# Three single passes of split operands for the up-projection behind the memory attention

## The reference

```python
def _L2_xattn_ref(query, keys):
    attn = softmax(einsum('bqd,bkd->bqk', 0.4 * query, 0.6 * keys))
    return einsum('bqk,bkd->bqd', attn, 0.6 * keys) + keys
def _L2_ffn_ref(x, W1, b1, theta, w_real, w_imag, W2, b2):     # 256 -> 1024 -> 256
    hidden = x @ W1 + b1
    imag = w_imag * sin(theta + hidden * 0.1)
    phase = cos(theta) * w_real + sin(theta) * w_imag
    return relu(hidden + phase * imag * 0.1) @ W2 + b2
x = x + _L2_xattn_ref(layernorm(x), ctx)
x = x + _L2_ffn_ref(layernorm(x), ...)
```

## Time and profile before

| | us |
|---|---|
| median of 3 runs | 2518.48 |
| lowest and highest run | 2516.29, 2525.79 |
| the profiled execution, device time | 2524.11 |
| its span, first to last instruction | 2522.3 |
| PE, DVE, ACT, POOL busy | 2247.0, 1665.1, 1316.9, 808.1 |

### The profile page before, as it was taken

The page is one execution under the profiler, slowest core; times in us unless marked ns, Lnnn a source line. Parts: engine busy times, 40 slices in busy tenths (PEclk is TensorE's granted clock), DMA queues, the critical chain, the costliest instruction groups (busy, mean ns, idle before and its releaser), DMA issues. The chain is left out here.

```text
span 2522.3 us, 48222 instructions
## 1 busy us (share of the span) xinstructions
PE 2247.0 (89%) x17198; PEld 1788.1 (71%) x17200; DVE 1665.1 (66%) x3232; ACT 1316.9 (52%) x3079; POOL 808.1 (32%) x1019
## 2 busy tenths in 40 slices
PE   6979799999698797989999979999789998899875
PEld 5857587887476796778888568888546567788752
DVE  5767635774566686764777456666567575888858
ACT  4558636664577563533666333333376464455335
POOL 4646502332355441100333102222210110454365
PEclk9989879999899899979999989999799999999988
DMA  3000082114200000050211420000200002777811
GB/s 112 2 1 2 10 334 77 51 51 170 101 2 1 22 2 1 2 239 31 107 52 52 173 105 1 1 2 1 101 1 1 1 1 68 224 218 208 238 29 34
DMA packets 102932, 178.35 MB, mean 71 GB/s; under 512 B 59687, under 2 KB 71591, under 8 KB 97578
## 3 DMA queue, kind: packets, MB, share of 16 engines
q1 hardware_dynamic: 85514, 135.93, 16.2%
q0 software_dynamic: 9792, 28.85, 3.6%
q10 hardware_dynamic: 7392, 10.49, 1.1%
HBM read 112.44 MB, written 62.78 MB: 69 GB/s over the span
## 5 line engine op out<-in xcount | busy, mean ns | idle before, releaser
L2289 POOL TENSOR_TENSOR l2a_Pn<-l2a_Pn,l2a_rden 128x1024 f32<-128x1024 f32 x32 | 60.0, 1897 | 295.3 <-DVE l2a_rden L2531 295.3
L1617 ACT ACTIVATE l0f_w_parts<-l0f_W 128x512 fp32r (+1 forms) x117 | 90.5, 775 | 64.7 <-PE l0f_psG L1422 50.4
L1768 DVE TENSOR_TENSOR l0f_w_parts<-l0f_W,l0f_w_parts 128x512 fp32r<-128x512 f32 (+1 forms) x117 | 99.2, 867 | 37.9 <-ACT l0f_w_parts L1617 37.8
L1617 ACT ACTIVATE l1f_w_parts<-l1f_W 128x512 fp32r (+1 forms) x117 | 90.4, 774 | 63.0 <-PE l1f_psG L1422 50.2
L4054 POOL TENSOR_TENSOR l3x_Pn<-l3x_Pn,l3x_fac 128x616 f32<-128x616 f32 (+2 forms) x96 | 70.3, 761 | 150.0 <-DVE l3x_fac L4133 140.6
L1768 DVE TENSOR_TENSOR l1f_w_parts<-l1f_W,l1f_w_parts 128x512 fp32r<-128x512 f32 (+1 forms) x117 | 99.2, 867 | 12.6 <-ACT l1f_w_parts L1617 12.2
L1475 PE MATMUL l1f_psY<-l1f_W,l1f_XT_hT 128*128 (+1 forms) x440 | 104.2, 380 | 0.8 <-ACT l1f_XT_hT L1597 0.8
L883 ACT ACTIVATE l1a_att_Pn<-l1a_att_psS,l1a_att_nmx 128x128 f32<-128x128 f32 x256 | 92.1, 422 | 1.7 <-DVE l1a_att_nmx L1002 1.7
L883 ACT ACTIVATE l0x_Pn<-l0x_psS,l0x_nmx 128x128 f32<-128x128 f32 x256 | 92.1, 422 | 0.9 <-DVE l0x_nmx L1002 0.9
L706 POOL TENSOR_TENSOR l1a_att_Pn<-l1a_att_Pn,l1a_att_rden 128x512 f32<-128x512 f32 x64 | 66.5, 1040 | 74.7 <-DVE l1a_att_rden L1009 74.7
L1475 PEld LDWEIGHTS l1f_psY<-l1f_W,l1f_XT_hT 128*128 128x128 f32 x440 | 80.3, 190 | 10.8 <-issue 1.0
(11 more groups left out here) (860 smaller groups left out, 7521.9 us busy)
## 6 DMA issues: line engine op xcount, KB each, us to landing
relative_rows<-l3x_ext SPq DMA_DIRECT2D x32, 516.0 KB, 5.8
l1f_W<-in_l1f_w SPq DMA_DIRECT2D x9, 1536.0 KB, 20.2
l0f_W<-in_l0f_w SPq DMA_DIRECT2D x8, 1536.0 KB, 26.4
cumulative_rows<-l3x_cum SPq DMA_DIRECT2D x32, 384.0 KB, 3.3
l3x_K<-keys SPq DMA_DIRECT2D x16, 512.0 KB, 5.5
l3x_rel<-relative_rows SPq DMA_DIRECT2D x32, 231.0 KB, 4.2
values<-l1f_W SPq DMA_DIRECT2D x11, 512.0 KB, 4.4
l3x_V<-values SPq DMA_DIRECT2D x16, 308.0 KB
```

What stands on the lines that cost most here:

```text
L1617: nc.scalar.activation(w_high[i], W[:, bass.ds(act_offsets[k] + o, m)], ACT.Copy).then_inc(high_ready, 1)
L1768: nc.vector.tensor_tensor(w_low[i], W[:, bass.ds(dve_offsets[k] + o, m)], w_high[i], ALU.subtract).then_inc(low_ready, 1)
L2289: nc.gpsimd.tensor_tensor(part, part, rden[b % 2][:, 8 * u:8 * u + 8].unsqueeze(2).to_broadcast([P, 8, P]), ALU.mult)\
```

## The change

The weights `w1` and the transposed tokens are each split in two parts of the type float32r, a rounded `high` and the rest `low`. `up(n)` becomes six matmuls of such parts in place of two of fp32: high·high, high·low and low·high for each half of the features. The product low·low is left out.

- `w1_high` and `w1_low` are new tiles. The loaded `w1` now lands in the first half of `aT[1]`, which is not in use before relu(8).
- `round_up_weights(c)` on ACT (128x1024, for c = 0 in step -5 and c = 1 in step -4) writes `w1_high`. It waits for the load of `w1`.
- `up_weight_residues(c)` on DVE (128x1024, in steps -4 and -1) writes `w1_low`. In step -1 it stands ahead of `coefficients`.
- `take_m` writes `xm_high`; `take_m_low` on DVE (128x512 from PSUM) writes `xm_low`. There are eight of each.
- `take_m(g, 1)` moves up in its step, from behind relu and take_pT to the place right behind turns; for g = 0 it stays where it was. `take_m_low(g, 1)` stands between rounded and fraction.
- PE waits for `xm_low_ready` wherever it waited for `xmT_ready`: ahead of the transposes that write `psA` again, and ahead of up(8g).

The diff, cut to its core:

```diff
-    w1, w2, b2 = R.sb("w1", [P, DC * F]), ...
+    w1_high, w1_low, w2, b2 = R.sb("w1_high", [P, DC * F], F32R), R.sb("w1_low", [P, DC * F], F32R), ...
-    xm, xmT = ring("xm", 2, 2 * D), ring("xmT", 2, DC * GT)
+    xm, xm_high, xm_low = ring("xm", 2, 2 * D), ring("xm_high", 2, DC * GT, F32R), ring("xm_low", 2, DC * GT, F32R)
     aT = ring("aT", 2, FC * GT)
+    w1 = aT[1][:, 0:DC * F]
...
         def transpose_m(g, r):
...
             past(pe, xmT_ready, n)
+            past(pe, xm_low_ready, n)
...
         def up(n):
             if n == 0:
-                pe.wait_ge(up_loaded, 16)
+                pe.wait_ge(w1_split, DC)
             pe.wait_ge(xmT_ready, 2 * g + 2)
+            pe.wait_ge(xm_low_ready, 2 * g + 2)
             for c in range(DC):
-                ins = nc.tensor.matmul(psH[n % 3][:, :], w1[:, c * F + j * P:c * F + (j + 1) * P], xmT[g % 2][:, c * GT:(c + 1) * GT],
-                                       start=(c == 0), stop=(c == DC - 1))
+                nc.tensor.matmul(psH[n % 3][:, :], w1_high[:, cols_], xm_high[g % 2][:, rows], start=(c == 0), stop=False)
+                nc.tensor.matmul(psH[n % 3][:, :], w1_high[:, cols_], xm_low[g % 2][:, rows], start=False, stop=False)
+                ins = nc.tensor.matmul(psH[n % 3][:, :], w1_low[:, cols_], xm_high[g % 2][:, rows], start=False, stop=(c == DC - 1))
...
+        def round_up_weights(c):
+            if c == 0:
+                act.wait_ge(up_loaded, 16)
+            nc.scalar.activation(w1_high[:, c * F:(c + 1) * F], w1[:, c * F:(c + 1) * F], ACT.Copy).then_inc(w1_rounded, 1)
...
+        def take_m_low(g, r):
+            n = 2 * g + r
+            dve.wait_ge(xmT_ready, n + 1)
+            past(dve, up_done, FC * (g - 1))
+            part = [t[g % 2][:, :].rearrange("p (c t) -> p c t", c=DC)[:, :, r * T2:(r + 1) * T2] for t in (xm_high, xm_low)]
+            nc.vector.tensor_tensor(part[1], psA[:, :].rearrange("p (c t) -> p c t", c=DC), part[0], ALU.subtract).then_inc(xm_low_ready, 1)
+
+        def up_weight_residues(c):
+            dve.wait_ge(w1_rounded, c + 1)
+            nc.vector.tensor_tensor(w1_low[:, c * F:(c + 1) * F], w1[:, c * F:(c + 1) * F], w1_high[:, c * F:(c + 1) * F], ALU.subtract)\
+                .then_inc(w1_split, 1)
```

More of the change, by code:

```diff
@@ L2634, in memory_attention_and_ffn @@
         "memory_read"))
-    stat_ready, ostd_ready, xm_ready, xmt_done, xmT_ready, x_biased = (R.sem(n) for n in (
-        "stats_ready", "memory_std_ready", "xm_ready", "xmT_done", "xmT_ready", "x_biased"))
+    stat_ready, ostd_ready, xm_ready, xmt_done, xmT_ready, xm_low_ready, x_biased = (R.sem(n) for n in (
+        "stats_ready", "memory_std_ready", "xm_ready", "xmT_done", "xm_high_ready", "xm_low_ready", "x_biased"))
+    w1_rounded, w1_split = R.sem("up_weights_rounded"), R.sem("up_weights_split")
     up_done, t_ready, k_ready, f_ready, sin_ready, q_ready, a_ready, y_done, x_ready = (R.sem(n) for n in (
@@ L2660, in _ @@
             sp.dma_start(t[:, :], A["l2f_" + n]).then_inc(vec_loaded, 16)
-        sp.dma_start(w1[:, :], A["l2f_W1"]).then_inc(up_loaded, 16)
+        sp.dma_start(w1, A["l2f_W1"]).then_inc(up_loaded, 16)
         load_context(GB, NB, ctx_loaded)
@@ L2675, in transpose_x @@
             past(pe, xmT_ready, max(0, 2 * ((q - 1) // 2)) if q >= 1 else 0)
+            past(pe, xm_low_ready, max(0, 2 * ((q - 1) // 2)) if q >= 1 else 0)
             for c in range(DC):
@@ L2811, in relu @@
             past(act, y_done, FC * (g - 2) + FC - 1 + j // (FC // 2))
+            if n == FC:
+                act.wait_ge(w1_split, DC)
             nc.scalar.activation(aT[g % 2][:, j * GT:(j + 1) * GT], qs[n % 2][:, :], ACT.Relu, bias=b1[:, j:j + 1]).then_inc(a_ready, 1)
@@ L2821, in _ @@
                 turns(k)
+            if k >= 0 and group_at(k, FC - 1) is not None:
+                take_m(group_at(k, FC - 1), 1)
             if 0 <= k - 1 < NK:
@@ L2831, in _ @@
                 memory_std(group_at(k, FC - 3))
-            for r in range(2):
-                if group_at(k, FC - 2 + r) is not None:
-                    take_m(group_at(k, FC - 2 + r), r)
+            if group_at(k, FC - 2) is not None:
+                take_m(group_at(k, FC - 2), 0)
+            if k == -1:
+                take_m(0, 1)
             if pair_at(k, 2) is not None:
                 exps(pair_at(k, 2))
+            if k in (-5, -4):
+                round_up_weights(k + 5)
         early_roots(nc, G, act, mv_ready, head_ready)
@@ L2963, in _ @@
                 rounded(k)
+                if group_at(k, FC - 1) is not None:
+                    take_m_low(group_at(k, FC - 1), 1)
                 fraction(k)
@@ L2972, in _ @@
                 maxima(pair_at(k, 2))
+            if k == -4:
+                up_weight_residues(0)
             if pair_at(k, 4) is not None:
@@ L2980, in _ @@
                 angles()
+            if group_at(k, FC - 2) is not None:
+                take_m_low(group_at(k, FC - 2), 0)
             if k == -1:
+                up_weight_residues(1)
                 coefficients()
+                take_m_low(0, 1)
             if NK - FC <= k < NK - FC + 10:
```

9 lines of the change are left out of this document (5 added, 4 removed).

## The result

| | before | after |
|---|---|---|
| median, us | 2518.48 (11 runs) | 2510.03 (11 runs) |
| lowest and highest run | 2514.10, 2525.79 | 2505.25, 2515.32 |
| ratio of the times, 95% interval | | 0.9963 (0.9953 to 0.9972) |
| span of the profiled execution | 2522.3 | 2506.6 |
| block's first DVE row | 1792.95 | 1785.65 |

What follows compares the result with a forecast made beforehand. It took ACT as the bound in steps 0 to 9, PE and ACT in turn in 10 to 22, PE alone from 23. Terms summed to 9.9 us won, from median 2518.48 to 2508.6 us; range 2504.5 to 2515.

Steps and rivals of the forecast that it cites:

- What a pass costs: Each up-projection: six passes 0.23 us apart, 1.39 us in all, making a PE-bound step 0.33 us shorter.
- turns(1) to turns(7): Early steps: ACT mostly the bound, only PE's wait at turns(5) shrinks; 0.3 us won.
- turns(9) to turns(15): Steps 11 to 13 give part of three times 0.33 us, steps 13 to 15 nothing; 0.8 us won.
- The lead-in, -0.7: Ahead of up(0): the last take_m_low delays it 0.69 us; the weight copies and first weight residue cost 0.
- The entry of group 1, 2.45: At up(8): moved copy starts it 1.5 us earlier, half-clock passes are shorter, clock still falls; 2.45 us won.
- Groups 2 and 3: At these entries the moved copy removes PE's waits: 1.3 us won at group 2, 0.2 at group 3.
- Steps 17 to 22: 0.33 us at five of six turns, less 0.15 where ACT is nearly full; 1.5 us won.
- From the sum to the time: Whole kernel: 5.6 us of the profiled execution set aside, the gain of 9.9 us subtracted from the median.
- (a): Clock stays up at group 1 and passes run at 0.216 us: gain 12.7 us; chance 0.17 for over 12.6.
- (b): Entries of groups 1 and 2 give nothing, so 2.45 and 1.3 us are lost: gain 6.15 us; chance 0.18.
- (c): PE idles more in steps and the clock falls, costing 2.9 us per half-clock bound step; chance 0.04.
- (d): Up-projection passes run as slowly as fp32 records, 0.86 us more each, 16 us in all; chance 0.02.

Runs made afterwards that it cites:

- e3: The changed kernel without the product of high weights and low tokens, so four passes per up-projection; ratio to the kernel before 0.9942.
- e2: The changed kernel with take_m(g, 1) and its residue back at their old places, so the passes alone; ratio to the kernel before 0.9989.
- e4: The changed kernel with fifteen more unread passes on PE at the entry of group 1; ratio to the kernel before 0.9956.
- e5: The changed kernel with the two low-token passes last and PE's wait for the token residue only ahead of them; ratio to the kernel before 0.9959.
- e9: The changed kernel with the low-token passes last and seven unread fp32 matmuls in PE's lead-in waits; ratio to the kernel before 0.9943.
- e7: The changed kernel with low-token passes last, seven unread matmuls in the lead-in and fifteen unread passes at group 1; ratio to the kernel before 0.9942.
- e1: The kernel before, still fp32, with only take_m(g, 1) moved right behind turns for groups 1 to 3; ratio to the kernel before 0.9986.
- e10: The kernel before, still fp32, with take_m(g, 1) right behind turns and seven unread matmuls in the lead-in; ratio to the kernel before 0.9957.

## Why the prediction was right, point by point

**What a pass costs: right.** 0.23 us apart, 1.39 for six, 3.11 a step. e3 confirms it with 2.65 for four passes. The 216 ns for an isolated matmul that the prediction named ("TensorE: Matmul & The Clock Gate" of the Trainium skill, "Back-to-back issue gap") is not reached: 1919.41 - 1919.18 = 0.23.

**The ladder.** Leads won in each stretch, the prediction's terms and the change's first profile:

| stretch | predicted | measured |
|---|---|---|
| to turns(1), lead-in included | 0.4 | 0.78 |
| turns(1) to turns(7) | 0.3 | 0.31 |
| turns(7) to turns(9), group 1 | 2.45 | 2.49 |
| turns(9) to turns(15) | 0.8 | 0.64 |
| turns(15) to turns(17), group 2 | 1.3 | 1.54 |
| turns(17) to turns(22) | 1.5 | 1.10 |
| step 23 | 0.3 | 0.21 |
| turns(23) to turns(31), group 3 included | 2.85 | 3.00 |
| sum | 9.9 | 10.07 |

*The lead-in, -0.7:* the step was right in kind and size. In e2, e3 and e4, where the clock rises as before, up(0) starts 0.73 us later and turns(1) leads by 0.39 to 0.42 where the change issues the same six passes; the forecast was 0.4. In the change itself an earlier rise of the clock gave the 0.73 back, which no step of mine held. It came in both profiles of the change, and not in e2 to e4 with the same work up to there. This is luck, worth 0.4 us at turns(1); without it the sum would be 9.7. The cover for the copies on ACT and for the first residue was there.

*The entry of group 1, 2.45:* right in the sum. PE's wait of 1.46 us, the order of copy, residue and up(8), and the clock's fall were as forecast. The fall came earlier than I had it, 53.7 us into the block and not at 57, behind the wait for the exponentials and not in the wait that I had followed, and so slowed transpose_m too.

*Groups 2 and 3:* right; PE's wait for the copy is gone in both. *Steps 17 to 22:* over-sized by 0.4, since only two of the five turns gave a full 0.33; the others gave 0.06, 0.25 and 0.12. The sum of 9.9 against 10.07 is closer than its terms, whose misses of +0.4, +0.2 and -0.4 cancel in part.

**From the sum to the time.** 5.6 us of the profiled execution were set aside as the stage's own. They turned up as such: its block was entered at 1792.95, and in the eleven profiles since, which share the code ahead of it but for line numbers, at 1784.85 to 1792.74. The times bear the sum out no closer than their interval, 7.1 to 11.8 us.

**The rivals.** (a) The clock did not stay up, and the passes did not run closer. Its premise is real, though. e4 shows that the fall costs 1.4 us of the block where I had 1.1 (e5: 1.5, e9 against e7: 1.0). (b) fell: e1 and e2 show the opposite, the order is the larger half. (c) did not happen in the change, but e2 shows its mechanism at group 2: with PE's wait at 2.06 us the clock fell in a bound step and 1.7 us went there, some 0.9 of them to the clock. With the copy moved this fall is in none of the kernels. The "one fall" in the trace of before, named there, counts from up(0) on; in its lead-in the clock also fell, about 2 and 19 us into the block. (d) fell with the first row of a pass.

**What the prediction did not see** is how the two parts depend on each other. It booked 4 us to the entries and 6 to the passes, as if each stood by itself. Measured, the order alone gives 5.61, with the clock up at group 1 in that one profile (in e10, also in fp32, it fell), the passes alone 2.96, and both together 10.07. With the copy at its old place the passes and their residue make PE wait longer ahead of the entries, 3.12 us where it was 3.02, 2.06 where it was 1.28 and 0.91 where it was 0.23.

## What to carry to other kernels

When a faster PE step stands in a stage where PE waits, look at each wait that the step leaves longer: the passes alone won 3 us, and an instruction moved by four places won more. Where an operand is split into a part that is ready early and one that is ready late, issue the passes of the early part first and wait for the other only ahead of its own; it took 0.7 us off PE's wait at each entry that was exposed. That shortens the block only where PE's chain is the bound: at up(0) it did, ahead of up(8), where ACT is the bound, it did not. Read small changes by the positions of the work in the profile, counted from the stage's start: the two profiles of the change enter this block 3.5 us apart, and all twelve, with the same code ahead of it, up to 8.1. And where a gain leans on the clock, repeat the profile: the clock fell in e9 and e10 at an entry where it had stayed up in e5 and e1.
